# Moving the last gating steps between the tiles of an expert layer, and one to three tiles earlier, in a fused attention and mixture-of-experts kernel

## The chip, the cores and the metric

One core of a Trainium2 chip. The metric is the device time of one execution in microseconds; lower is better. It is taken as the median of several executions.

## The reference, cut to what matters

Two layers in float32 over 32 sequences of 128 tokens, width 128: cross attention with 16 heads to a context of 77 tokens, then a feed-forward layer of 8 experts of which each token takes the best 2.

```python
x = x + xattn(layernorm(x), ctx, ctx, W_q, b_q, W_k, b_k, W_v, b_v, W_o, b_o, mask)
n = layernorm(x)
pn = l2norm(n @ Wp.T);  sn = l2norm(sim_matrix)
gate_scores = pn @ sn.T / temperature
top_v, top_i = top_k(gate_scores, 2)
comb = sum(one_hot(top_i) * softmax(top_v)[..., None], axis=-2)
h  = gelu(n @ W1[e] + b1[e])            # for each expert e
eo = h @ W2[e] + b2[e]
x = x + sum_e eo[e] * comb[..., e]
```

## The kernel before, in words

The attention runs over 16 pairs of sequences (J = 0 to 15, NP = 16), as a software pipeline in which each engine has its own written order (step). At the end of a pair's pipeline stand the gating steps. TensorE turns the normalised rows (turn), multiplies them with the gate weights (gate) and counts how many earlier tokens chose the same expert (rank, count_rows). ScalarE copies and squares (turned, gated). VectorE adds the attention's result to x (residual), takes its mean and variance (second_stats, second_mean), normalises it into rows (second_norm), picks the best two experts (gates, best, best_places, one_hots, chosen, chosen_sum, chosen_sums) and makes from the ranks the row numbers in the experts' lists (ranks, rows_of_lists, rows_taken). GpSimd takes the powers -1/2 (second_power for the norm, gate_power for the gate's length, signalled as rn_ready) and scatters each pair's rows, four indirect DMAs per pair, into lists in DRAM (scatter).

Then 71 tiles of 128 rows (N_TILES = 71) go through the expert layer. Tile j uses the weights of one expert, whose number comes from a table. The tables are made in two parts: part 0, for the first 41 tiles, before the tiles start, and part 1 from the counts of all pairs, in 14 small VectorE stages (tables(1, stage)), one step on TensorE (tables(1)) and the copies back on VectorE (table_rows(1), which ends with the instruction into tab_b that brings tab_ready to 5). The attention's last pairs are not done when the tiles start: the gating of pairs 14 and 15 and the tables of part 1 run among tiles 0 to 20.

Each engine has a function for one tile. An engine works through its instructions in the order written, and a wait holds up all that stands behind it.

- TensorE, tile(j): transpose the rows of tile j+2 (L767), the 8 "up" matmuls of tile j+1 (L774, they wait for xtT of j+1, w1c of j+1 and h of j-1), the 8 "down" matmuls of tile j-1 (L785, they wait for hT of j-1 and eo of j-3).
- VectorE, tile(j): eo of tile j-1 (L1703, after its down), the copy xtT of tile j+3 (L1709, after its transpose), then h of tile j+2 (L1725, after its up).
- ScalarE, tile(j): the weight copy w1c of tile j+2 (L1189), then the gelu hT of tile j (L1193).
- GpSimd, give_back(j): the row numbers didx of tile j+1 (places, L579), then the indirect DMA that scatters eo of tile j into results (L590), then a memset that spaces these DMAs (L593). A list scatter (L457) among them is followed by a longer memset (spread, L527).
- SyncE loads the rows of a tile into a ring of 8 buffers: tile j+8 is loaded when didx of tile j has been computed and its rows were transposed (L395 to L399).

The helper steps (L315) calls between(j) ahead of tile(j) for the tiles up to the start of its loop; the loop starts at tile 20 on VectorE, 21 on TensorE and ScalarE, 22 on GpSimd. On TensorE, ScalarE and GpSimd the gating steps are in between(j) before the change. On VectorE they are in beside(j), which tile(j) calls in its middle, after the copy xtT and ahead of h (L1710). TensorE and ScalarE wait for tab_ready = 5 ahead of their tile 21, VectorE ahead of its tile 20.

Of the kernel before, what the change touches and what calls it, by code (L numbers as in the profile page):

```python
# [6 lines left out]
def xattn_moe_kernel(nc, x, ctx, mask, w_q, b_q, w_k, b_k, w_v, b_v, w_o, b_o,  # L7
# [26 lines left out]
    NP = NB // 2  # L34
# [26 lines left out]
    LOOPED = 20  # L61
# [15 lines left out]
    with est:  # L77
# [207 lines left out]
        def known(b):  # L285
            return isinstance(b, int)
# [17 lines left out]
        def settled(eng):  # L304

            eng.nop(nofuse=True)
# [113 lines left out]
        def _(pool):  # L421
# [173 lines left out]
            def between(j):  # L595
                if j == 0:
                    second_power(NP - 1, NP - 1)
                elif j in (7, 9, 11, 13):
                    k = (7, 9, 11, 13).index(j)
                    scatter(NP - 2, NP - 2, k // TOPK, k % TOPK)  # L600
                    spread(5 + k)
                elif j == 6:
                    gate_power(NP - 1, NP - 1)
                    destinations(NP - 1, NP - 1)
                elif j in (15, 17, 19, 21):
                    k = j // 2 - 7
                    scatter(NP - 1, NP - 1, k // TOPK, k % TOPK)
                    spread(9 + k)
                elif j == LOOPED + 2:
                    pool.wait_ge(skip_ready, 2)  # L610
# [17 lines left out]
        def _(pe):  # L628
# [424 lines left out]
            project(15)  # L1053

            def between(j):
                if j == 4:
                    after(pe, E["dots_ready"], NP - 2)
                    rank(NP - 2, NP - 2)
                elif j == 5:
                    after(pe, E["x2_ready"], NP - 1)  # L1060
                    turn(NP - 1, NP - 1)
                elif j == 6:
                    after(pe, E["rk_ready"], NP - 2)
                    gate(NP - 1)
                elif j == 12:
                    after(pe, E["dots_ready"], NP - 1)
                    count_rows(NP - 1, ps_x[:, COUNTED])
                    rank(NP - 1, NP - 1)
                elif j == 20:
                    after(pe, E["xn2T_ready"], NP - 1)  # L1070
                    tables(1)
                elif j == 21:
                    pe.wait_ge(tab_ready, 5)
# [5 lines left out]
        def _(act):  # L1079
# [224 lines left out]
            tile(0, 0)  # L1304

            def between(j):
                if j == 5:
                    turned(NP - 1)
                elif j == 7:
                    gated(NP - 1, NP - 1)  # L1310
                elif j == LOOPED + 1:
                    act.wait_ge(tab_ready, 5)
# [29 lines left out]
        def _(dve):  # L1342
# [49 lines left out]
            def residual(J):  # L1392
                after(dve, E["o_done"], J)
                after(dve, E["xb_ready"], J)
                nc.vector.tensor_tensor(pair(x2, J), ps_o[:, 256:512], pair(x2, J), ALU.add).then_inc(E["x2_ready"], 1)  # L1395
# [65 lines left out]
            def best_places(J):  # L1461
                after(dve, E["top_ready"], J)
                settled(dve)
                for s in range(2):
                    last = nc.vector.max_index(idx8[:, s, :], top8[:, s, :], gv[:, s, :])
                last.then_inc(E["idx_ready"], 1)
                dcol = diff[:, 2 * J:2 * J + 2] if known(J) else diff[:, bass.ds(J * 2, 2)]
                nc.vector.tensor_tensor(dcol, top8[:, :, 1], top8[:, :, 0], ALU.subtract).then_inc(E["diff_ready"], 1)

            def one_hots(J):  # L1470
                after(dve, E["idx_ready"], J)
                nc.vector.tensor_tensor(ohs[:, :, :, :], iota_e[:, 0:NE].unsqueeze(1).unsqueeze(1).to_broadcast([P, 2, TOPK, NE]),
                                        idx8[:, :, 0:TOPK].unsqueeze(3).to_broadcast([P, 2, TOPK, NE]), ALU.is_equal
                                        ).then_inc(E["ohs_ready"], 1)
# [164 lines left out]
                nc.vector.scalar_tensor_tensor(x2[:, b, :], ys[:, b // CH, 1, b % CH, :], p2[:, b:b + 1], x2[:, b, :],  # L1639
                                               ALU.mult, ALU.add).then_inc(sum2, 1)  # L1640

            def beside(j):
                if j == 0:
                    best_places(NP - 2)
                    one_hots(NP - 2)
                elif j == 1:
                    residual(NP - 1)
                    second_stats(NP - 1)
                    second_mean(NP - 1, NP - 1)
                elif j == 2:  # L1650
                    chosen(NP - 2)
                    chosen_sum(NP - 2, NP - 2)
                    chosen_sums(NP - 2, NP - 2)
                elif j == 3:
                    second_norm(NP - 1, NP - 1)
                elif j == 4:
                    ranks(NP - 2)
                    rows_of_lists(NP - 2)
                    rows_taken(NP - 2, NP - 2)
                elif 5 <= j < 8:  # L1660
                    chances(0, j - 5)
                elif j == 8:
                    gates(NP - 1, NP - 1)
                    best(NP - 1)
                elif j == 9:
                    best_places(NP - 1)
                    one_hots(NP - 1)
                elif j == 10:
                    chosen(NP - 1)
                    chosen_sum(NP - 1, NP - 1)  # L1670
                    chosen_sums(NP - 1, NP - 1)
                elif j == 12:
                    ranks(NP - 1)
                    tables(1, 0)
                    tables(1, 1)
                elif j == 13:
                    rows_of_lists(NP - 1)
                    rows_taken(NP - 1, NP - 1)
                    tables(1, 2)
                elif 14 <= j < 17:  # L1680
                    tables(1, 2 * j - 25)
                    tables(1, 2 * j - 24)
                elif j == 17:
                    tables(1, 9)
                    tables(1, 10)
                    tables(1, 11)
                elif j == 18:
                    tables(1, 12)
                    tables(1, 13)
                elif j == 19:  # L1690
                    table_rows(1)

            def tile(j, m):
                t = j - 1 + AHEAD
                if has(j, -1, N_TILES) or has(t, 0, N_TILES):
                    both = dve.value_load(tab_b[0:1, t:t + 1] if known(t) else tab_b[0:1, bass.ds(t, 1)],
                                          min_val=0, max_val=33 * (NE - 1) * FC)
                    e1, e2 = both % 32, both // 32 * (D // FC)
                if has(j, -1, N_TILES):
                    q = (m - 1) % FRING  # L1700
                    after_dma(dve, returned, j - 1 - FRING, q)
                    after_tile(dve, FE["down_done"], j - 1)
                    nc.vector.tensor_tensor(eo[:, q, :], ps_s[:, 2 + (m - 1) % 2, 0:D], b2s[:, bass.ds(e2, D)], ALU.add  # L1703
                                            ).then_inc(FE["eo_ready"], 1)
                if has(j, 3, N_TILES):
                    r = (m + 1) % 2
                    after_tile(dve, FE["up_done"], j + 1)
                    after_tile(dve, FE["xtT_done"], j + 3)
                    nc.vector.tensor_copy(xtT[:, r, :], turned_rows(j + 3, r)).then_inc(FE["xtT_ready"], 1)  # L1709
                if known(j):  # L1710
                    beside(j)
                if known(j) and N_TILES - EARLY <= j < N_TILES:
                    b = j - (N_TILES - EARLY)
                    if b == 0:
                        dve.wait_ge(p_step, 3)
                    if b % CH == 0:
                        after_y(dve, b // CH)
                    first_sum(b)
                    if b > 0:
                        second_sum(b - 1)  # L1720
                if has(j, 2, N_TILES):
                    r = m % 2
                    after_tile(dve, FE["act_ready"], j)
                    after_tile(dve, FE["up_done"], j + 2)
                    nc.vector.tensor_tensor(h[:, r, :].rearrange("p (c t) -> p c t", c=FC),  # L1725
                                            ps_s[:, r, :].rearrange("p (c t) -> p c t", c=FC),
                                            b1T[:, bass.ds(e1, FC)].unsqueeze(2).to_broadcast([P, FC, P]), ALU.add
                                            ).then_inc(FE["h_ready"], 1)
# [155 lines left out]
            best(14)  # L1884
            context(15)
            tile(0, 0)

            def between(j):
                if j == LOOPED:
                    dve.wait_ge(tab_ready, 5)  # L1890

            steps(dve, tile, 1, N_TILES, LOOPED, N_TILES - EARLY - 1, FRING, between)
# [40 lines left out]
```

## Time and profile before

| | |
|---|---|
| median of 3 executions | 378.75 us (377.77 to 378.83) |
| profiled execution | 377.77 us, span from first to last instruction 376.0 us |
| TensorE (PE) busy | 342.3 us, 91% of the span |
| VectorE (DVE) busy | 306.0 us, 81% |
| ScalarE (ACT) busy | 290.3 us, 77% |
| GpSimd (POOL) busy | 271.9 us, 72% |
| mean granted TensorE clock | 0.978 of full speed |

The profile comes from one execution, the 377.77 us one. Times in its rows count from the first instruction. A row of a timeline gives start, length, engine, line, instruction, and, in brackets, how long the engine sat idle before it and what ended that. The chain of waits follows the last instruction back to what released each step. The attention takes the span up to about 209 us; TensorE's tiles run from there to 353 us, and the remainder is the last results' way back through DRAM and the sum.

### The profile page before, as it was taken

The numbers are of one execution on the slowest core, as the hardware profiler recorded it, in microseconds if no ns is written. First come the engines' busy times: TensorE is split into PE (matmuls) and PEld (weight loads), VectorE is DVE, ScalarE is ACT, GpSimd is POOL, SyncE is SP. The second block draws the span as 40 slices with busy tenths as digits, with TensorE's granted clock in tenths as the row PEclk, the third lists the DMA queues.
The fourth block names the chain that finished last, engine by engine and source line by source line (L and its number), as shares of the span: only waits on it lengthen the run. The fifth ranks groups of instructions, "written<-read, shape, count | busy, mean of one in ns | idle before, by whom it ended". The sixth has DMA issues, their size and how long they took to land.

```text
span 376.0 us, 14240 instructions
## 1 busy us (share of the span) xinstructions
PE 342.3 (91%) x3584; PEld 288.8 (77%) x3585; DVE 306.0 (81%) x972; ACT 290.3 (77%) x847; POOL 271.9 (72%) x506
## 2 busy tenths in 40 slices
PE   7899999999999999999998899999999999999900
PEld 3467777777777777777776699999889999999900
DVE  6778999999999999999999787786556666668884
ACT  4899999999999999999987857665556666666621
POOL 7532487777777877777755468899888878687773
PEclk9999999999999999999999999999999999999965
DMA  3122123321331211120000212222232222249247
GB/s 93 45 82 80 32 72 102 102 64 61 103 97 63 59 44 44 52 72 22 22 25 30 68 45 74 67 68 72 74 86 80 76 71 70 70 133 285 62 117 218
DMA packets 42567, 29.16 MB, mean 78 GB/s; under 512 B 5443, under 2 KB 39311, under 8 KB 42528
## 3 DMA queue, kind: packets, MB, share of 16 engines
q1 hardware_dynamic: 34992, 18.60, 18.3%
q0 software_dynamic: 4320, 8.53, 6.8%
q10 hardware_dynamic: 3216, 1.57, 1.5%
q8 instruction: 16, 0.26, 0.3%
q14 instruction: 23, 0.19, 0.2%
HBM read 17.53 MB, written 11.62 MB: 78 GB/s over the span
## 4 chain that ended last, share of the span: by engine, by line
PE 54%; DVE 22%; issue 10%; POOL 4%; ACT 3%; DMA 3%; DVEq 2%; POOLq 0%; SPq 0%; ACTq 0%
PE ps_s L774 14%; PE ps_s L785 14%; PE ps_t L665 6%; PE ps_o L676 5%; PE ps_s L649 4%; DVE sums L1373 4%; DVE mx L1356 3%; PE ps_s L639 3%; DVE rows L1441 2%; PE ps_t L767 2%; PE ps_x L696 2%; DVE pr L1366 2%; DMA ys<-results 1%; DVE x L1395 1%; DVE st L1405 1%
## 5 line engine op out<-in xcount | busy, mean ns | idle before, releaser
L590 POOL DMA_INDIRECT results<-eo,didx x71 | 70.7, 996 | 19.8 <-issue 13.2
L457 POOL DMA_INDIRECT lists<-rows,slots x64 | 66.7, 1042 | 17.8 <-issue 16.4
L785 PE MATMUL ps_s<-w2s,hT 128*128 x568 | 75.8, 277 | 0.1
L774 PE MATMUL ps_s<-xtT,w1c 128*128 128x128 f32 x568 | 75.5, 276 | 0.0
L1091 ACT ACTIVATE pT<-ps_t 77x512 f32<-77x512 f32 x128 | 73.8, 594 | 0.9 <-PE ps_t L665 0.9
L665 PE MATMUL ps_t<-identf,pr 128*77 128x128 f32 x512 | 72.7, 275 | 0.4 <-ACT pT L1091 0.3
L785 PEld LDWEIGHTS ps_s<-w2s,hT 128*128 128x128 f32 x568 | 69.1, 192 | 0.8 <-issue 0.4
L1189 ACT ACTIVATE w1c<-w1s 128x512 f32 x71 | 44.7, 630 | 31.9 <-PE ps_s L774 29.4
L774 PEld LDWEIGHTS ps_s<-xtT,w1c 128*128 128x128 f32 x568 | 69.0, 192 | 0.1
L1725 DVE TENSOR_TENSOR h<-ps_s,b1T 128x512 f32<-128x512 f32 x71 | 49.1, 691 | 19.4 <-PE ps_s L774 18.7
L665 PEld LDWEIGHTS ps_t<-identf,pr 128*77 128x77 f32 x512 | 58.6, 147 | 6.8 <-issue 4.6
L1193 ACT ACTIVATE hT<-h 128x512 f32<-128x512 f32 x71 | 44.7, 629 | 18.5 <-DVE h L1725 14.2
L1356 DVE TENSOR_REDUCE mx<-ps_s 128x8 f32<-128x616 f32 x64 | 48.1, 792 | 8.4 <-PE ps_s L649 8.3
L1366 DVE TENSOR_TENSOR pr<-ps_s,mx 128x308 f32<-128x308 f32 (+1 forms) x64 | 40.1, 630 | 0.1
L1131 ACT ACTIVATE pr<-ps_s,mx 128x77 f32<-128x77 f32 x128 | 39.8, 329 | 0.4 <-DVE mx L1356 0.2
L1703 DVE TENSOR_TENSOR eo<-ps_s,b2s 128x128 f32<-128x128 f32 x71 | 20.7, 292 | 23.0 <-PE ps_s L785 17.7
L676 PE MATMUL ps_o<-pT,vpad 77*32 77x128 f32 x1024 | 34.6, 276 | 4.0 <-ACT recT L1179 4.0
L1373 DVE TENSOR_REDUCE sums<-pr 128x12 f32<-128x924 f32 x32 | 35.4, 1105 | 0.0
L676 PEld LDWEIGHTS ps_o<-pT,vpad 77*32 77x32 f32 x1024 | 26.0, 109 | 10.6 <-ACT recT L1179 7.6
L520 POOL TENSOR_TENSOR kbd<-kT,headmask 128x616 f32<-128x616 f32 x16 | 19.4, 1213 | 15.4 <-ACT kT L1155 15.3
L1131 ACT ACTIVATION_READ_ACCUMULATOR pr<-ps_s,mx 128x1 f32 x128 | 26.9, 210 | 0.0
L649 PE MATMUL ps_s<-kbd,qT 32*128 32x308 f32 x256 | 25.6, 470 | 0.4 <-ACT qT L1173 0.4
(220 smaller groups left out, 621.3 us busy)
## 6 DMA issues: line engine op xcount, KB each, us to landing
xt<-lists SPq DMA_DIRECT2D x71, 66.0 KB, 1.9
ys<-results SPq DMA_DIRECT2D x14, 256.0 KB, 4.0
xin<-in_x_dram SPq DMA_DIRECT2D x16, 128.0 KB
w1s<-in_L_ffn_W_dram SPq DMA_DIRECT2D x8, 256.0 KB
w2s<-in_L_ffn_W_dram SPq DMA_DIRECT2D x8, 256.0 KB
out_dram<-x SPq DMA_DIRECT2D x5, 256.0 KB, 6.0
cin<-in_ctx_dram SPq DMA_DIRECT2D x16, 77.0 KB
results<-eo,didx POOLq DMA_INDIRECT x71, 2.4
```

Of the source, the lines that this page charges most:

```text
L457: nc.gpsimd.indirect_dma_start(lists, bass.IndirectOffsetOnAxis(ap=slots[:, r, s * TOPK + k:s * TOPK + k + 1], axis=0), rows[:, r, s, k, : ...
L590: nc.gpsimd.indirect_dma_start(results, bass.IndirectOffsetOnAxis(ap=didx[:, r:r + 1], axis=0), eo[:, r, :], None, bounds_check=TOPK * NTO ...
L665: last = nc.tensor.transpose(ps_t[0:SK, g % 2, j * P:(j + 1) * P], pr[:, s, g * HG + j, :], identf[:, :])
L676: last = nc.tensor.matmul(ps_o[g * QR:(g + 1) * QR, s * P:(s + 1) * P], vpad[0:SK, r, s * G + g, j * QR:(j + 1) * QR], pT[0:SK, g, j * P:( ...
L774: last = nc.tensor.matmul(ps_s[:, r, c * P:(c + 1) * P], w1c[:, r, c * P:(c + 1) * P], xtT[:, r, :], start=True, stop=True)
L785: last = nc.tensor.matmul(ps_s[:, 2 + r, 0:D], hT[:, r, c * P:(c + 1) * P], w2s[:, bass.ds(e + c * D, D)], start=(c == 0), stop=(c == FC - 1))
L1091: nc.scalar.activation(pT[0:SK, g, :], ps_t[0:SK, g % 2, :], ACT.Copy).then_inc(E[f"t{g}_ready"], 1)
L1131: last = nc.scalar.activation(pr[:, s, hd, :], ps_s[:, 3, (hd - HB) * SK:(hd - HB + 1) * SK], ACT.Exp, bias=mx[:, s, hd:hd + 1], accum_out ...
L1356: nc.vector.tensor_reduce(grouped(mx[:, s, n * HG:(n + 2) * HG]), bank(n, 2), AX.X, ALU.max, negate=True).then_inc(E["maxA" if n == 0 else ...
L1366: nc.vector.tensor_tensor(pr[:, s, hd, :].rearrange("p (n h) k -> p n h k", h=HG), bank(n, nb), grouped(mx[:, s, hd]).unsqueeze(3).to_broa ...
L1373: nc.vector.tensor_reduce(sums[:, m % 2, s, 0:HB], pr[:, s, 0:HB, :], AX.X, ALU.add).then_inc(E["sums_ready"], 1)
L1725: nc.vector.tensor_tensor(h[:, r, :].rearrange("p (c t) -> p c t", c=FC), ps_s[:, r, :].rearrange("p (c t) -> p c t", c=FC), b1T[:, bass.d ...
```

## The change: what it does

VectorE's function beside is taken away. Its steps go into between(j), ahead of the whole tile(j), so that they stand behind h of the tile before instead of ahead of h of this tile. Those of pair 14's choice (best_places to chosen_sums) and pair 15's residual, statistics and mean all come right behind tile(0). The second norm of pair 15 moves from tile 3 to ahead of tile 2, the row numbers of pair 14 from tile 4 to ahead of tile 3, chances from 5 to 7 to ahead of 4 to 6. The steps from gates(15) on keep their number j and stand ahead of the tile; the tables' stages are dealt out anew, and table_rows(1) goes from the middle of tile 19 to ahead of tile 20.

TensorE's rank(14), turn(15), gate(15) and count_rows and rank(15) come one tile earlier, as do ScalarE's turned(15) and gated(15). GpSimd's scatters of pair 14 go from ahead of tiles 7, 9, 11, 13 to ahead of 3, 4, 7, 9, and those of pair 15 from 15, 17, 19, 21 to 14, 16, 18, 20. Its gate_power(15) stays ahead of tile 6.

```diff
 GpSimd, between(j)
-                elif j in (7, 9, 11, 13):
-                    k = (7, 9, 11, 13).index(j)
+                elif j in (3, 4, 7, 9):
+                    k = (3, 4, 7, 9).index(j)
                     scatter(NP - 2, NP - 2, k // TOPK, k % TOPK)
                     spread(5 + k)
                 elif j == 6:
                     gate_power(NP - 1, NP - 1)
                     destinations(NP - 1, NP - 1)
-                elif j in (15, 17, 19, 21):
+                elif j in (14, 16, 18, 20):
 TensorE, between(j)
-                if j == 4:
+                if j == 3:
                     after(pe, E["dots_ready"], NP - 2)
                     rank(NP - 2, NP - 2)
-                elif j == 5:
+                elif j == 4:
                     after(pe, E["x2_ready"], NP - 1)
                     turn(NP - 1, NP - 1)
-                elif j == 6:
+                elif j == 5:
                     after(pe, E["rk_ready"], NP - 2)
                     gate(NP - 1)
-                elif j == 12:
+                elif j == 11:
                     after(pe, E["dots_ready"], NP - 1)
                     count_rows(NP - 1, ps_x[:, COUNTED])
                     rank(NP - 1, NP - 1)
 ScalarE, between(j)
-                if j == 5:
+                if j == 4:
                     turned(NP - 1)
-                elif j == 7:
+                elif j == 6:
                     gated(NP - 1, NP - 1)
 VectorE, tile(j)
-                if known(j):
-                    beside(j)
 VectorE, after tile(0, 0)
+            best_places(14)
+            one_hots(14)
+            chosen(14)
+            chosen_sum(14, 14)
+            chosen_sums(14, 14)
+            residual(15)
+            second_stats(15)
+            second_mean(15, 15)
 
             def between(j):
-                if j == LOOPED:
+                if j == 2:
+                    second_norm(NP - 1, NP - 1)
+                elif j == 3:
+                    ranks(NP - 2)
+                    rows_of_lists(NP - 2)
+                    rows_taken(NP - 2, NP - 2)
+                elif 4 <= j < 7:
+                    chances(0, j - 4)
+                elif j == 8:
+                    gates(NP - 1, NP - 1)
+                    best(NP - 1)
+                elif j == 9:
+                    best_places(NP - 1)
+                    one_hots(NP - 1)
+                elif j == 10:
+                    chosen(NP - 1)
+                    chosen_sum(NP - 1, NP - 1)
+                    chosen_sums(NP - 1, NP - 1)
+                elif j == 12:
+                    ranks(NP - 1)
+                    tables(1, 0)
...
+                elif j == LOOPED:
+                    table_rows(1)
                     dve.wait_ge(tab_ready, 5)
```

## Rows read from the trace of the kernel before

**Rows 1.** Windows: stretch, length, busy us of each engine, PE clock, DMA share, GB/s
```profile
223.00:256.00 33.00, 32.79 (x292) 32.32 (x292) 26.37 (x97) 21.79 (x40) 29.26 (x56) 1.00 0.25 71
256.00:276.00 20.00, 18.32 (x149) 17.11 (x148) 10.79 (x31) 10.24 (x18) 18.05 (x35) 1.00 0.24 70
276.00:300.00 24.00, 24.00 (x215) 23.81 (x214) 14.73 (x37) 15.69 (x26) 21.17 (x45) 1.00 0.30 84
```

**Rows 2.** Chain that ended last, around 271 to 274 us: start, length, what
```profile
271.29 0.15 POOL didx L579
...
272.32 1.86 DMA xt<-lists
...
274.23 0.33 PE ps_t L767
```

**Rows 3.** Timeline of GpSimd (POOL): start, length, instruction, idle time before it and its releaser
```profile
221.61 0.19 POOL L496 TENSOR_SCALAR ve<-mv 128x2 f32<-128x2 f32 x1 [2.10 <-DVE mv L1414]
...
222.94 1.05 POOL L590 DMA_INDIRECT results<-eo,didx  x1 [0.17 <-POOL didx L579]
...
226.24 0.99 POOL L590 DMA_INDIRECT results<-eo,didx  x1 [0.16 <-DVE eo L1703]
...
231.55 0.99 POOL L590 DMA_INDIRECT results<-eo,didx  x1 [0.58 <-issue]
...
233.27 0.72 POOL L509 TENSOR_TENSOR rn<-n2c,neghalf 128x2 f32<-128x2 f32 x1
...
239.41 1.00 POOL L590 DMA_INDIRECT results<-eo,didx  x1 [0.16 <-POOL didx L579]
...
242.63 0.99 POOL L590 DMA_INDIRECT results<-eo,didx  x1 [0.16 <-DVE eo L1703]
```

**Rows 4.** Timeline of VectorE (DVE), tiles 0 to 2
```profile
218.13 0.08 DVE L1465 MATCH_VALUE_LOAD idx<-top,gv 128x8 f32 x1
...
218.77 0.69 DVE L1725 TENSOR_TENSOR h<-ps_s,b1T 128x512 f32<-128x512 f32 x1
...
220.01 0.41 DVE L1395 TENSOR_TENSOR x<-ps_o,x 128x256 f32<-128x256 f32 x1
...
221.45 0.69 DVE L1725 TENSOR_TENSOR h<-ps_s,b1T 128x512 f32<-128x512 f32 x1
...
222.70 0.17 DVE L1479 TENSOR_TENSOR sel<-ohs 128x16 bf16<-128x16 f32 x1
```

**Rows 5.** Timeline of TensorE (PE); L767 opens a tile
```profile
221.11 1.06 PE L774 MATMUL ps_s<-xtT,w1c 128*128 128x128 f32 x8
...
223.28 0.17 PE L702 MATMUL ps_x<-sel,tri 128*128 128x16 bf16 x1 [0.21 <-DVE selsum L1485]
...
231.97 0.27 PE L767 MATMUL ps_t<-identf,xt 128*128 128x128 f32 x1
...
233.86 0.27 PE L767 MATMUL ps_t<-identf,xt 128*128 128x128 f32 x1
...
239.82 0.30 PE L767 MATMUL ps_t<-identf,xt 128*128 128x128 f32 x1
...
255.65 0.28 PE L767 MATMUL ps_t<-identf,xt 128*128 128x128 f32 x1
...
280.57 0.27 PE L767 MATMUL ps_t<-identf,xt 128*128 128x128 f32 x1
```

**Rows 6.** Timeline of VectorE, tiles 8 and 19
```profile
234.64 0.48 DVE L1451 TENSOR_SCALAR gv<-dots,rn 128x8 f32<-128x8 f32 x2
...
256.24 0.17 DVE L1602 TENSOR_SCALAR bias_at<-ps_o 1x33 f32<-1x33 f32 x1
...
256.69 0.17 DVE L1612 SCALAR_TENSOR_TENSOR tab_b<-bias_at 1x33 int32<-1x33 f32 x1
257.07 0.69 DVE L1725 TENSOR_TENSOR h<-ps_s,b1T 128x512 f32<-128x512 f32 x1 [0.20 <-PE ps_s L774]
```

**Rows 7.** Timeline of ScalarE (ACT), tile 21
```profile
257.82 0.63 ACT L1189 ACTIVATE w1c<-w1s 128x512 f32 x1 [1.75 <-DVE tab_b L1612]
```

More of the change, by code:

```diff
@@ L1640, in second_sum @@
                                                ALU.mult, ALU.add).then_inc(sum2, 1)
[L1642 to L1691, printed above, removed]
             def tile(j, m):
@@ L1886, in _ @@
             tile(0, 0)
-            def between(j):
-                if j == LOOPED:
+            best_places(14)
[6 more added lines that the diff above has]
+            second_mean(15, 15)
+            def between(j):
+                if j == 2:
[19 more added lines that the diff above has]
+                    tables(1, 0)
+                elif j == 13:
+                    rows_of_lists(NP - 1)
+                    rows_taken(NP - 1, NP - 1)
+                    tables(1, 1)
+                elif 14 <= j < 17:
+                    tables(1, 2 * j - 26)
+                    tables(1, 2 * j - 25)
+                elif 17 <= j < 19:
+                    tables(1, 3 * j - 43)
+                    tables(1, 3 * j - 42)
+                    tables(1, 3 * j - 41)
+                elif j == LOOPED:
+                    table_rows(1)
                     dve.wait_ge(tab_ready, 5)
```

## The prediction

> **What bounds the kernel now.** I read the windows first, then the chain, then the timelines of the four engines over tiles 0 to 30. I write P8 for the start of TensorE's tile 8, its L767 row; G5 for the start of GpSimd's L590 of tile 5; a dash (P8') for the same thing after the change. The windows split the edited region in two [rows 1]. From 223 to 256 us TensorE is busy 32.79 of 33 us: it never waits for VectorE there, and a tile costs 233.86 - 231.97 = 1.895 us [rows 5]. From 256 to 276 it is busy 18.32 of 20, while GpSimd has 18.05; after 276 it is full again up to the last tile. The chain says what the waits of the middle window are [rows 2]: didx of tile 22 on GpSimd at 271.29, then the load of tile 30, which lands at 274.18, then TensorE's tile 28. GpSimd had been working without a break from 221.61, where it had waited 2.10 us for the mean of pair 15 [rows 3]. So the ring of 8 buffers, paced by GpSimd, sets TensorE's time at tile 28, and TensorE, which with 1.895 us a tile would have been there earlier, has slack before it. From P12 = 239.82 to P20 = 255.65 are 15.83 us [rows 5]; 8 more tiles of 1.895 would bring P28 to 270.8. It came at 274.23 [rows 2]: the slack is 3.4 us. The time after P31 = 280.57 [rows 5] follows TensorE one to one. The change's worth is therefore the shift of P31.
>
> **The GpSimd chain.** It starts with the mean of pair 15. VectorE's rows price the moved steps, from one start to the next [rows 4]: the places and one-hots 218.77 - 218.13 = 0.64 us; the three chosen steps 0.65 (222.70 to TensorE's rank at 223.28, which needs two of them [rows 5], and a third like them, an estimate); residual, statistics and mean 221.45 - 220.01 = 1.44. Before, h of tile 2 stood behind the places and started at 218.77; now it starts at 218.13 and takes 0.62, then come 0.64 + 0.65 + 1.44. The mean is ready at 221.5 us instead of 221.45. Nothing is gained there: the chosen steps that went ahead of it cost what tile 1's eo and xtT cost before. The work on GpSimd's queue up to G21 stays the same: 22 returns at (226.24 - 222.94) / 2 = 1.65 us or a little less, 8 scatters that each make 1.6 more (242.63 - 239.41 = 3.22 with one [rows 3]), and gate_power. All eight stand ahead of G21 in both orders. The only term is the 0.58 us of idle time ahead of G5 [rows 3], of which 0.4 is beyond the usual; it may go or stay. So the ring allows P28' between 273.8 and 274.3.
>
> **VectorE, tiles 0 to 6.** The xtT copy of tile 4 used to be done for TensorE's up at 221.11 [rows 5]; now it stands behind all the steps of the last paragraph: mean at 221.5, about 0.4 for register work, eo, then xtT, done near 222.4. TensorE waits 1.3 us. It wins back the wait at rank(14) (223.28, [rows 5]), since chosen is done by 220.1. Then up and down of tile 3 take 1.8, and turn, gate and two tiles as before (P6 = 231.97 - 2 x 1.895 = 228.18, less 223.28, less 0.2 for rank, 4.7): P6' = 222.45 + 1.8 + 4.7 = 228.95, which is 0.8 late. The moves of second_norm and of ranks(14) cost nothing: their inputs are there 1 us ahead, and an op of up to 1.1 us between h and eo delays xtT by less than TensorE has in hand.
>
> **The order of gates(15).** GpSimd now has two scatters ahead of G3 and G4, and gate_power(15) still stands ahead of G6. G5' = G2 + 3.22 + 3.22 + 1.63 = 226.24 + 8.07 = 234.3, against 231.55. The power ends 233.27 + 0.72 - 231.55 = 2.44 behind it [rows 3]: 236.75, against 233.99. VectorE's gates(15) stand ahead of its tile 8, where VectorE arrives at 234.9 (P8' = 232.75, and h comes 1.4 us behind the tile's start: 257.07 - 255.65 [rows 5, 6]), so it waits 2 us with eo of tile 7, xtT of tile 11 and h of tile 10 queued behind. gates take 0.48 (L1451, [rows 6]) and best with the gaps about as much again, 0.85 together as an estimate, then eo, then xtT at 238.7. TensorE wanted it at P10' = 228.95 + 4 x 1.895 = 236.5. It waits 2.1 us, so P10' acts as 238.65. Before, the same wait had 0.65 in hand (gates at 234.64 [rows 6] against 233.99).
>
> **The order of count_rows(15).** TensorE wants the three chosen sums at the end of tile 10 (ahead of tile 11). VectorE does them ahead of its tile 10, which is behind h of tile 11, and that h needs TensorE's up of tile 10. So: P10' + 1.4 (h) + 0.6 + 0.65 + 0.15 = P10' + 2.8, where TensorE is free at P10' + 1.9. That is a wait of 0.9 whatever came before, and the places of pair 15, still late from the last paragraph, add about 0.4. P11' = 238.65 + 2.8 + 0.4 + 0.3 (count and rank) = 242.15, P12' = 244.1, P20' = 244.1 + 15.83 = 259.9.
>
> **The order of table_rows.** Before, it took 256.24 to 256.86, ahead of h of tile 21 at 257.07 [rows 6], and TensorE's tile 21, at P20 + 1.9 = 257.55, came behind it and did not wait. Now it is behind that h: P20' + 1.42 + 0.62 + 0.62 = P20' + 2.66. TensorE, free at P20' + 1.9, waits for it ahead of its tile 21 and then has the loop's head and its register work to do, which took ScalarE 257.82 - 256.86 = 0.96 [rows 6, 7]; I take 0.45 for TensorE, between 0.15 (a bare wake-up) and 0.96. P21' = P20' + 3.1 = 263.0. w1c of tile 23 comes at P20' + 3.6 and is wanted at P20' + 5: hidden.
>
> **The sum.** P31' = 263.0 + 10 x 1.895 = 281.95, and about 0.25 for the first tile behind a wait, which runs slower (P12 to P20 before held 0.1 of it): 282.2, against 280.57. The shift is +1.6 us. The ring asks only for 274.3 at P28' (276.3 here), so it no longer binds. The profiled execution would go from 377.77 to 379.4, the median, 0.98 above it before, from 378.75 to 380.35. I say 380.3.
>
> **The rivals.** (B) TensorE's waits are covered by its slack. They sum to 0.8 + 2.1 + 1.3 + 1.2 = 5.4 against 3.4 of slack and 0.6 of slow tiles that went with the waits before. If gates(15) finds its power 1.5 us sooner, or the loop heads are free, P28' is the ring's 274.2 and the time 378.7. For: the sum exceeds the slack by little, and each term is worked out to some 0.3 us. Against: three terms would have to be too large at once. (D) Faster: the waits stay small, GpSimd's 0.4 us goes, and TensorE, with no wait at tile 28, skips the slow tiles that followed it (280.57 - 274.23 = 6.34 for three tiles of 1.895, 0.65 lost). P31' = 273.8 + 5.7 = 279.5, time 377.7. It decides where the power of pair 15 is done by 235 us. Against: GpSimd had no idle time from which the scatters could be paid. (C) Slower: the waits reach GpSimd. Its return at 226.24 was released by eo of tile 2 [rows 3], and VectorE is late there by up to 0.8 us; with that the power, gates and all behind move too, and each wait leaves 0.4 of slow tiles: +3, 381.8. (E) The TensorE clock falls in a wait and 2 to 3 tiles run at half speed: +4 to +6 us beside the rest, near 384.5. The rows speak against it: the granted clock stayed at 1.00 through the window with 1.68 us of waits [rows 1], though none alone was as long as 2 us.
>
> The Trainium skill (TensorE: Matmul & The Clock Gate, Part 1, "What's actually happening") says that an idle TensorE is set back to 1.2 GHz, the lower of two levels, and that activity releases it; by that rule (E) is possible if a wait counts as idle, and gives its 384.5. No row here has a wait of 2 us inside the tiles, so the trace leaves it open; the window at 1.00 is nearest and I follow it.
>
> **How the numbers follow.** Chances: forecast 0.55 (own range 379.4 to 381.4), B 0.23, C 0.11, D 0.07, E 0.04. A measurement of this kernel tells about 0.3% (1.1 us) from no change. Slower by more: four fifths of the forecast, C and E, 0.6. Faster: half of D and the tail of B, 0.07. The remaining 0.33 is the same. The range goes from B's low side, 378.2, to C's 381.9.
>
> **What would show it.** Right: VectorE idle 1.5 to 2.5 us ahead of gv (L1451) with the power on GpSimd as releaser; TensorE waiting near 241 us for the sums ahead of L709 and for tab_b ahead of tile 21; no wait for xt loads at tiles 22 to 28; P31 near 282. Wrong: if TensorE still waits for xt at tile 28 near 274, the ring has kept the bound; if P6 is before 228.2 or gv has no wait, my order of arrival is wrong.

## The result and the profile after

The changed kernel takes 384.2 us (383.54 to 385.56) against 378.69 for the kernel before; the ratio is 1.0155, 95% interval 1.0119 to 1.0191. It is 5.5 us slower, where 1.6 were forecast; the range ended at 381.9. The profiled execution took 386.43 us, its span is 384.6; it is the slowest of the eleven executions of this measurement (382.83 to 386.43), so its rows show more of a loss than the median does.

TensorE of the kernel after (start, length, instruction, idle time before it and its releaser). Against [rows 5]:

```profile
224.23 1.16 PE L774 MATMUL ps_s<-xtT,w1c 128*128 128x128 f32 x8 [1.48 <-DVE xtT L1658]
...
238.24 0.27 PE L767 MATMUL ps_t<-identf,xt 128*128 128x128 f32 x1
241.18 1.16 PE L774 MATMUL ps_s<-xtT,w1c 128*128 128x128 f32 x8 [2.66 <-DVE xtT L1658]
242.26 1.87 PE L785 MATMUL ps_s<-w2s,hT 128*128 x8
244.64 0.17 PE L709 MATMUL ps_x<-selsum,onesb 128*128 128x8 bf16 x1 [0.51 <-DVE selsum L1490]
...
245.17 1.94 PE L774 MATMUL ps_s<-xtT,w1c 128*128 128x128 f32 x8
...
250.85 0.27 PE L767 MATMUL ps_t<-identf,xt 128*128 128x128 f32 x1
...
266.45 0.28 PE L767 MATMUL ps_t<-identf,xt 128*128 128x128 f32 x1
...
269.52 0.32 PE L767 MATMUL ps_t<-identf,xt 128*128 128x128 f32 x1 [0.94 <-DVE tab_b L1612]
...
288.91 0.27 PE L767 MATMUL ps_t<-identf,xt 128*128 128x128 f32 x1
```

The first row is the up of tile 4 (the matmuls of L774), which stood at 221.11 before; it waits 1.48 us for xtT. At 241.18 the up of tile 11 waits 2.66 us; behind it the groups of eight take 1.87 and 1.94 us where they took 1.06. L709 waits for the sums, the transpose at 269.52 for tab_b, and P31 is 288.91 against 280.57. No transpose waits for a load at tiles 22 to 28 any more.

VectorE of the same kernel, against [rows 4, 6]:

```profile
222.83 0.25 DVE L1414 BATCH_NORM_AGGREGATE mv<-st 128x2 f32<-128x6 f32 x2
223.69 0.29 DVE L1652 TENSOR_TENSOR eo<-ps_s,b2s 128x128 f32<-128x128 f32 x1 [0.61 <-issue]
...
225.34 0.28 DVE L1652 TENSOR_TENSOR eo<-ps_s,b2s 128x128 f32<-128x128 f32 x1
...
239.31 0.36 DVE L1451 TENSOR_SCALAR gv<-dots,rn 128x8 f32<-128x8 f32 x2 [2.75 <-POOL rn L509]
...
240.63 0.29 DVE L1652 TENSOR_TENSOR eo<-ps_s,b2s 128x128 f32<-128x128 f32 x1 [0.62 <-issue]
...
257.99 0.15 DVE L1564 TENSOR_TENSOR upto<-done,todo 128x16 f32<-128x16 f32 x1
258.78 0.29 DVE L1652 TENSOR_TENSOR eo<-ps_s,b2s 128x128 f32<-128x128 f32 x1 [0.63 <-issue]
...
260.25 0.16 DVE L1571 TENSOR_REDUCE which<-cmp 128x1 f32<-128x16 f32 x1
261.05 0.29 DVE L1652 TENSOR_TENSOR eo<-ps_s,b2s 128x128 f32<-128x128 f32 x1 [0.64 <-issue]
```

gv (L1451) waits 2.75 us for the power. A row that the forecast had not: eo (L1652) stands 0.6 us in "issue", time in which the engine waits for nothing that the profile shows, behind most of the moved steps (223.69, 240.63, 258.78, 261.05). Behind the second norm, whose instruction takes 0.73 us, it does not (225.34).

GpSimd, against [rows 3]: the chain starts at 223.27, the return of tile 2 at 228.68 (G2'), that of tile 5 at 236.76 (G5', forecast 234.3), the power at 238.49.

```profile
223.27 0.19 POOL L496 TENSOR_SCALAR ve<-mv 128x2 f32<-128x2 f32 x1 [2.72 <-DVE mv L1414]
...
228.68 0.99 POOL L590 DMA_INDIRECT results<-eo,didx  x1 [0.56 <-issue]
...
236.76 0.99 POOL L590 DMA_INDIRECT results<-eo,didx  x1 [0.16 <-issue]
...
238.49 0.72 POOL L509 TENSOR_TENSOR rn<-n2c,neghalf 128x2 f32<-128x2 f32 x1
```

The windows, against [rows 1]; columns as there, the granted clock third from the end:

```profile
223.00:256.00 33.00, 28.60 (x225) 27.92 (x226) 18.72 (x70) 16.43 (x32) 26.61 (x51) 0.90 0.22 60
256.00:276.00 20.00, 18.36 (x151) 16.76 (x150) 13.12 (x48) 10.67 (x18) 17.42 (x33) 1.00 0.24 67
```

From 223 to 256 TensorE has 28.60 of 33 us where it had 32.79, and 225 matmuls instead of 292: it waits 4.2 us more, and its clock is at 0.90 of full speed. Four shorter windows show where:

```profile
238.00:241.00 3.00, 0.52 (x5) 0.28 (x3) 0.96 (x6) 0.31 (x1) 2.65 (x7) 1.00 0.16 44
241.00:244.00 3.00, 2.82 (x16) 2.55 (x16) 2.32 (x12) 1.26 (x2) 2.67 (x5) 0.75 0.24 70
244.00:247.00 3.00, 2.49 (x14) 2.33 (x14) 0.91 (x6) 0.63 (x1) 2.67 (x6) 0.50 0.31 89
247.00:250.00 3.00, 3.00 (x19) 3.00 (x19) 1.18 (x3) 1.26 (x2) 2.14 (x6) 0.61 0.27 65
```

From 244 to 247 us the granted clock is 0.50, the lower level, 1.2 GHz; TensorE had waited 2.66 us before it fell.

TensorE's tile starts in the two profiled executions place the loss:

| stretch | before | after | difference | forecast |
|---|---|---|---|---|
| up to P3 | 221.00 | 222.45 | +1.45 | 0 |
| P3 to P9 | 12.86 | 13.90 | +1.04 | +0.8 |
| P9 to P13 | 7.95 | 14.50 | +6.55 | +3.4 |
| P13 to P20 | 13.84 | 15.60 | +1.76 | 0 |
| P20 to P21 | 1.90 | 3.07 | +1.17 | +1.2 |
| P21 to P31 | 23.02 | 19.39 | -3.63 | -3.8 |
| sum at P31 | | | +8.34 | +1.6 |

The first line lies ahead of every instruction that the change moves: TensorE's tiles start 0.7 us later (210.56 against 209.86) and the first load of rows comes 0.7 later still. It is left out of the account. In the four profiles of the changed kernel and its versions taken next the tiles start 0.4 to 0.7 us later than in the one profile of the kernel before, so whether all of it is chance stays open.

### The profile page after: what moved, and what is told of

The parts are those of the page before. It is cut to its first block, busy times and chain, and to the rows that moved or that the text cites. A ratio compares the mean times of both kernels' runs of the same rounds, so it can differ in the third digit from the quotient of the medians.

```text
span 384.6 us, 14240 instructions
## 1 busy us (share of the span) xinstructions
PE 346.2 (90%) x3584; PEld 291.7 (76%) x3585; DVE 305.0 (79%) x972; ACT 290.7 (76%) x847; POOL 272.2 (71%) x506
## 4 chain that ended last, share of the span: by engine, by line
PE 52%; DVE 24%; issue 11%; POOL 3%; ACT 3%; DVEq 3%; DMA 3%; SPq 1%; POOLq 0%; ACTq 0%
PE ps_s L774 14%; PE ps_s L785 13%; PE ps_t L665 6%; PE ps_o L676 4%; DVE sums L1373 3%; PE ps_s L649 3%; DVE mx L1356 3%; PE ps_s L639 2%; DVE rows L1441 2%; DVE h L1672 2%; PE ps_t L767 2%; PE ps_x L696 1%; DMA ys<-results 1%; DVE pr L1366 1%; DVE x L1395 1%
## 5 line engine op out<-in xcount | busy, mean ns | idle before, releaser
L774 PE MATMUL ps_s<-xtT,w1c 128*128 128x128 f32 x568 | 77.0, 279 | 4.8 <-DVE xtT L1658 4.6
L785 PE MATMUL ps_s<-w2s,hT 128*128 x568 | 76.9, 280 | 0.1
L774 PEld LDWEIGHTS ps_s<-xtT,w1c 128*128 128x128 f32 x568 | 70.2, 195 | 6.3 <-DVE xtT L1658 6.2
L785 PEld LDWEIGHTS ps_s<-w2s,hT 128*128 128x128 f32 x568 | 70.6, 196 | 0.6 <-issue 0.4
L1652 DVE TENSOR_TENSOR eo<-ps_s,b2s 128x128 f32<-128x128 f32 x71 | 20.7, 292 | 28.6 <-issue 14.3
```

Source lines behind the costliest of these rows:

```text
L774: last = nc.tensor.matmul(ps_s[:, r, c * P:(c + 1) * P], w1c[:, r, c * P:(c + 1) * P], xtT[:, r, :], start=True, stop=True)
L785: last = nc.tensor.matmul(ps_s[:, 2 + r, 0:D], hT[:, r, c * P:(c + 1) * P], w2s[:, bass.ds(e + c * D, D)], start=(c == 0), stop=(c == FC - 1))
```

## The experiments

The runs were made in five series, each with the kernel before beside the others. Ratios are to the kernel before of the same series, with 95% intervals. In the first series (after_again to load_first) the kernel before took 379.0 us, and the parts can be priced to 0.5 us. In the other four it took 387 to 394. The chains of nine of the fourteen traces taken there hold pauses of 1.1 to 4.4 us that no instruction explains (no trace of the kernel before was taken there); those series tell only what is larger than some 0.3%.

**The control, after_again.** No edit.

> The changed kernel once more, as control for the runs beside it. Theory (four costs add up: VectorE's wait for the power of pair 15, 2.8 us; the TensorE clock that falls in that wait, about 2.8; register work of VectorE that lies open behind each moved step, about 2.3; the waits for the chosen sums and for tab_b, about 2): 384.2, with the same waits at the same tiles. Rival (part of the 5.5 us is scatter between executions, as the attention ended 0.7 us later in the one profile taken): this profile lies at 383 or less, with the attention as before.

386.16 us where 384.2 were expected, before 378.98: ratio 1.019 (1.0174 to 1.0205). The waits stand at the same tiles to 0.02 us. The rival falls: its tiles start 0.4 us late in the profile, and the loss was larger, 7.2 us. All executions here had a mean granted clock of 0.969 or 0.970. Of the eleven of the first measurement, the four at 0.970 or 0.971 took 385.6 to 386.4, the seven at 0.975 to 0.978 took 382.8 to 384.6.

**fill: keep TensorE busy in the wait.**

```diff
+                elif j == 10:
+                    warm_up(10)
                 elif j == 11:
```

> The changed kernel with ten matmuls of 512 columns on the constant ones, into a bank that nobody reads then, on TensorE ahead of its tile 10, where it otherwise waits 2.8 us for xtT of tile 11. Theory (the fall of the clock behind that wait is a cost of its own): the wait of VectorE's gv for the power stays at about 2.8 us, the granted clock stays at 1.00, the groups of 8 behind it take 1.06 instead of 1.87 to 1.94, and the time falls by 2.5 to 3 us to 381.5. Rival (VectorE and GpSimd set the pace there, the slow matmuls are covered): groups at 1.06 but the time stays within 0.5 us of 384.2.

383.92 us, 2.2 less than the control; ratio 1.0128 (1.0108 to 1.0149). TensorE of this kernel:

```profile
237.08 2.32 PE L931 MATMUL ps_o<-onesb 128*128 128x512 bf16 x10
...
240.10 1.16 PE L774 MATMUL ps_s<-xtT,w1c 128*128 128x128 f32 x8 [0.59 <-DVE xtT L1660]
241.19 1.15 PE L785 MATMUL ps_s<-w2s,hT 128*128 x8
243.57 0.17 PE L709 MATMUL ps_x<-selsum,onesb 128*128 128x8 bf16 x1 [1.23 <-DVE selsum L1492]
```

and its window 244 to 247, with the clock at 1.00 where it was 0.50:

```profile
244.00:247.00 3.00, 3.00 (x28) 3.00 (x28) 1.67 (x5) 1.26 (x2) 2.67 (x6) 1.00 0.25 75
```

The groups of eight matmuls are back at 1.1 and P9 to P13 takes 12.54 us instead of 14.50. The fall of the clock is a cost of its own, 2 us in executions like those of the control; the 2.5 to 3 expected were a little high, as a second wait, 1.23 us at L709 instead of 0.51, took some back.

**pool_order: the scatters of pair 14 back.**

```diff
-                elif j in (3, 4, 7, 9):
-                    k = (3, 4, 7, 9).index(j)
+                elif j in (7, 9, 11, 13):
+                    k = (7, 9, 11, 13).index(j)
```

> The changed kernel with GpSimd's scatters of pair 14 back ahead of tiles 7, 9, 11 and 13, so that gate_power(15) is no longer behind two of them. Theory: gv's wait of 2.8 us goes, with it the idle stretch in which the clock fell, and about 0.4 us at the chosen sums: 6 us less if nothing else binds, of which the ring and the remaining waits leave about 4 us: 380.3. Rival (the order of the scatters is not the cause, the late start of GpSimd's chain behind the mean of pair 15 is): gv still waits over 1 us and the time stays above 383.

380.56 us, 5.6 less than the control, 0.3 from the expected time; ratio 1.0044 (1.003 to 1.0058). The power comes at 234.69 (GpSimd) and gv no longer waits (VectorE):

```profile
234.69 0.72 POOL L509 TENSOR_TENSOR rn<-n2c,neghalf 128x2 f32<-128x2 f32 x1
```

```profile
235.52 0.36 DVE L1451 TENSOR_SCALAR gv<-dots,rn 128x8 f32<-128x8 f32 x2
```

The rival falls, and the order of the scatters is shown as the cause of the long wait. P9 to P13 takes 9.79 us. TensorE's tiles 16 to 18 still take 2.3 to 2.5 us each.

**load_first: the steps behind the register read.**

```diff
                     e1, e2 = both % 32, both // 32 * (D // FC)
+                if known(j):
+                    ahead_of_eo(j)      # the steps of between(j), 2 <= j < 19
```

> The changed kernel with VectorE's steps of between(j) done inside tile(j), behind the read of the expert's offset from tab_b into a register and ahead of eo, instead of ahead of that read. Same steps, same places against eo, xtT and h. Theory (behind a step the register read lies open, 0.6 us per tile, and makes VectorE's tiles 15 to 20 2.3 to 2.4 us long, above TensorE's 1.895): the idle time of 0.6 ahead of eo goes in those tiles, TensorE's tiles 16 to 19 are back at 1.9, and the time falls by 2 to 2.5 us to about 382. Rival (the steps themselves are too long to fit behind h): tiles of 2.3 stay, the time falls by less than 0.5.

380.14 us, 6.0 less than the control where 2 to 2.5 were expected; ratio 1.0032 (1.0018 to 1.0047). VectorE of this kernel, behind the last steps ahead of two tiles:

```profile
252.44 0.15 DVE L1564 TENSOR_TENSOR upto<-done,todo 128x16 f32<-128x16 f32 x1
252.59 0.29 DVE L1688 TENSOR_TENSOR eo<-ps_s,b2s 128x128 f32<-128x128 f32 x1
...
254.19 0.16 DVE L1571 TENSOR_REDUCE which<-cmp 128x1 f32<-128x16 f32 x1
254.30 0.29 DVE L1688 TENSOR_TENSOR eo<-ps_s,b2s 128x128 f32<-128x128 f32 x1
```

eo follows 0.15 and 0.11 us behind the start of the last step, against 0.79 and 0.80 in the kernel after (257.99 to 258.78, 260.25 to 261.05). P13 to P20 takes 13.84 us, exactly the time of the kernel before: 1.76 of the 6.0. Most of the rest is in P9 to P13, 11.01 instead of 14.50 (0.9 came ahead of tile 9, 0.5 of it ahead of tile 3, where the code is the same), and TensorE's rows say why it is more than the 0.6 of one register read:

```profile
238.80 1.16 PE L774 MATMUL ps_s<-xtT,w1c 128*128 128x128 f32 x8 [1.71 <-DVE xtT L1694]
239.79 1.06 PE L785 MATMUL ps_s<-w2s,hT 128*128 x8
```

The up of tile 11 waits 1.71 us instead of 2.66: the power came 0.35 us sooner against the tile's start (gv waits 2.42 instead of 2.75), and from gv to eo are 0.70 us instead of 1.32. The groups behind the wait take 1.16 and 1.06: the clock stayed up in all four executions (0.978 to 0.980). So part of the 6.0 is the clock's 2 us, which fill had priced. Stretch by stretch against the kernel before, in the order of the table above, load_first has +0.41, +0.65, +3.06, 0, +1.15 and -3.73, and P31 at 282.11, where the forecast had 282.2.

**order_load: both edits at once**, in three series, as they were disturbed.

> The changed kernel with both of the last two edits: scatters of pair 14 back ahead of tiles 7 to 13, and VectorE's steps behind the register read. Theory (the costs of the order on GpSimd and of the open register read are separate terms): tiles 17 to 19 on TensorE go from 2.3 to 2.5 us back to 1.9, 1.6 us in all, on top of the 5.6 that the order gave: 378.9, what is left over being the wait for xtT of tile 4, the chosen sums and tab_b, under the ring's slack. Rival (the two edits repair the same loss, each took 5.6 to 6 us alone): 380.1, no better than either.

> The kernel with both edits (scatters of pair 14 back, steps behind the register read) again: in the last call the kernel before itself took 393.7 instead of 378.9, and engines stood still up to 5 us in places that no wait of the program explains, so its differences of 1 us could not be read. Theory (order and register read are separate terms): before + 0 to 0.3, 379.0. Rival (they repair the same loss): 380.1, before + 1.2.

> Scatters of pair 14 back and VectorE's steps behind the register read. Theory A (separate terms): before + 0 to 0.3, as nothing over the ring's slack is left. Theory B (both repair the same loss, the idle stretch in which the clock fell, and the rest is the waits for the sums and tab_b): before + 1.2, as each alone.

Ratios 1.0039 (1.001 to 1.0068), 1.006 (1.0032 to 1.0088) and 1.0037 (1.0017 to 1.0057), medians 395.04, 395.9 and 388.74. Theory A, before + 0.3 at most, is outside all three intervals. Theory B, before + 1.2 (1.003), is inside two and just below the third: the two edits repair mostly the same loss, the long wait with the clock's fall behind it, and 1.3 to 2.6 us stay above before. How much of that is these series' own pauses is not told apart.

**all_back: both edits, and with them count_rows(15) and rank(15) ahead of tile 12 and table_rows(1) in the middle of tile 19.**

```diff
-                elif j == 11:                    # TensorE
+                elif j == 12:
+                if known(j) and j == LOOPED - 1: # VectorE, tile(j), behind xtT
+                    table_rows(1)
```

> As the kernel with both edits, and with count_rows and rank of pair 15 back ahead of TensorE's tile 12 and table_rows(1) back in the middle of VectorE's tile 19. Theory (the waits of 0.9 to 1.2 us for the chosen sums and of 1.2 us for tab_b are the last two terms; behind them the ring, paced by GpSimd, binds as in the kernel before): TensorE's tiles 11 and 21 at 1.9, waits for xt near tiles 22 to 28 again, 378.9 to 379.1, equal to before. Rival (the waits were all that held it, and the earlier placing pays): 1.5 us below before, 377.4.

> The kernel with all four edits again, for the same reason. Theory (nothing but the ring is left): equal to before within 0.3 us, with waits for xt near tiles 22 to 28. Rival (early placing pays): 1.5 us below before.

> All four edits. Theory: the waits for the sums (0.9) and for tab_b (1.2) go, TensorE's tiles 11 and 21 take 1.9 to 2.2; where h2 was above before by them, this is equal to before within 0.3, and the ring binds again. Rival: 1.5 below before.

> All four edits, beside it. Theory: equal to start_only within 0.3 us, since only the start is left of the change's costs. Undisturbed, both are at before + 0 to 0.3.

Ratios 1.0018 (0.9991 to 1.0046), 1.0029 (1.0006 to 1.0053), 1.0033 (1.001 to 1.0056) and 1.0019 (0.9999 to 1.004). Each is 0.2 to 0.3% above before, two of them clear of noise and two not: the rival, that the earlier placing pays 1.5 us, falls, and the theory, equal to before within 0.3 us (0.0008), is inside three of the intervals and just outside the other. What the waits for the sums and for tab_b cost alone is not told apart here, since order_load and all_back overlap in all three series in which both ran.

**pool_only: GpSimd's part of the change alone on the kernel before.**

```diff
-                elif j in (7, 9, 11, 13):
+                elif j in (3, 4, 7, 9):
-                elif j in (15, 17, 19, 21):
+                elif j in (14, 16, 18, 20):
```

> The kernel before with GpSimd's part of the change alone: all eight scatters where the change has them. Theory (the late power costs what stands behind VectorE's wait for it; in the old place, in the middle of tile 8, eo of tile 7 and xtT of tile 11 are already done and only h of tile 10 is behind it): gv waits about 2 us, TensorE waits 0.5 us or less, the slack covers it: 379.0, the same as before. Rival (the late power is enough by itself): TensorE waits 2 us near its tile 10, the clock falls, 381 or more.

> GpSimd's part of the change alone on the kernel before, again. Theory (only what stands behind VectorE's wait counts, and in the middle of tile 8 that is h alone): gv waits about 2 us, TensorE at tiles 10 and 11 about 0.5, and the time is before within 0.3. Rival (the late power is enough): TensorE waits 2 us and more and the time is before + 2. In the disturbed call gv waited 1.7 and the time was equal to before.

Ratios 0.9983 (0.9954 to 1.0011) and 0.9992 (0.9973 to 1.001): no difference, as expected. In the two profiles gv waited 1.72 and 0.48 us, less than the 2.75 of the kernel after. TensorE's up of tile 12 in the second waited 0.45 us:

```profile
242.35 1.16 PE L774 MATMUL ps_s<-xtT,w1c 128*128 128x128 f32 x8 [0.45 <-DVE xtT L1709]
```

In the first it waited 1.00. So the new order of the scatters costs nothing that can be measured where only h stands behind gv, and in the changed kernel, where eo and xtT do, taking it back gave 5.6 us. These series are those with the pauses; the chain of the first profile shows one, on VectorE between a register instruction and the next wait:

```profile
256.14 0.02 DVEq L1696
256.17 2.27 another core or an unknown queue
...
258.46 0.02 DVEq L294
```

**no_spread: the kernel before without the spacing memsets.**

```diff
                     scatter(NP - 2, NP - 2, k // TOPK, k % TOPK)
-                    spread(5 + k)
...
-                    spread(9 + k)
```

> The kernel before without the eight spacing memsets (spread) behind the list scatters of pairs 14 and 15, 0.46 us each on GpSimd's chain. Theory (GpSimd's queue, through the ring of 8 buffers, holds TensorE at tiles 22 to 28): the chain is 3.7 us shorter, the waits for xt go, TensorE's tiles 22 to 30 take 1.9 and the time falls by 3 to 4 us to 375.3. Rival (the spacing is needed, closer scatters make the DMAs or the instruction issue slower by as much, or TensorE is the bound): 378 to 379.

> The kernel before without the eight spacing memsets behind list scatters, again. Theory (GpSimd's chain through the ring binds): 375.3. Rival (without the spacing GpSimd's DMA issues slow down, as the disturbed call had it, 5 us above before with 18 us of idle time of GpSimd ahead of its returns): before or above, 379 to 384.

> The kernel before without the eight spacing memsets behind list scatters. Theory (GpSimd's chain through the ring binds in an undisturbed execution): 3 to 4 us below before, TensorE's tiles 22 to 28 at 1.9. Rival (seen in two disturbed calls: GpSimd stands 1.3 to 2.8 us ahead of some returns once the spacing is gone): 0 to 4 us above before.

Ratios 1.0111 (1.0079 to 1.0142), 1.0108 (1.0081 to 1.0135) and 1.0163 (1.0118 to 1.0209). The theory falls for these executions: it is slower, by 4.6 to 6 us. GpSimd of the last, two returns:

```profile
248.74 1.00 POOL L590 DMA_INDIRECT results<-eo,didx  x1 [2.26 <-issue]
...
257.84 1.00 POOL L590 DMA_INDIRECT results<-eo,didx  x1 [1.97 <-issue]
```

With the 0.46 us memset gone, three returns up to 260 us stand 1.2 to 2.8 us in "issue" in each of the three traces; up to 260 us no other trace of these series has one over 1.4. But the chain that ended last goes through something else. In all three traces it holds a pause of 4.1 to 4.4 us on VectorE behind the last of pair 15's chosen sums, which is most of the loss; in the last:

```profile
242.18 4.33 another core or an unknown queue
```

In the other eleven traces of these series no pause on the chain is over 2.4 us. What it is, and whether GpSimd's issues or this pause cost the time, was not tested, and no undisturbed series has this version, so whether GpSimd's chain can be shortened is open.

**start_only: the steps right behind tile 0, alone on the kernel before**; and the changed kernel in a disturbed series.

```diff
             tile(0, 0)
+            best_places(14)
+            one_hots(14)
...
+            second_mean(15, 15)
```

> The kernel before with one part of VectorE's move alone: places, one-hots and chosen of pair 14 and residual, statistics and mean of pair 15 right behind tile 0; all else in its old place. Theory: TensorE's step from tile 3 to tile 4 takes 3.2 to 3.6 us instead of 2.4 (4.4 where registers are slow), GpSimd's chain starts 0.2 us later; the ring covers the first and leaves 0.2: before + 0 to 0.3 us undisturbed, and + 1 where the disturbed chips have no slack. Rival (the start costs nothing, what was left in all_back is the register read): before within 0.1% on any chip.

> The changed kernel as control beside the three others. Theory: before + 5.5 to 7, depending on how long the clock stays low in an execution.

start_only: ratio 0.9995 (0.9964 to 1.0026), its ten executions from 390.4 to 397.3; two of them, at a mean clock of 0.969, took 396.7 and 397.3, above every execution of the kernel before (392.2 to 395.2). That shows no cost in the median, but the interval ends at + 1.0 us: the theory's + 1 is at its very edge and the + 0 to 0.3 of an undisturbed chip well inside, so neither it nor the rival is settled (all_back beside it stood 1.0 us higher, within the noise of both), and what makes the 0.2 to 0.3% of all_back stays open. h1_after: 390.33 against 387.43, ratio 1.0075 (1.0048 to 1.0103), 2.9 us, less than the 5.5 to 7 expected; its clock was low for two groups of eight, behind a wait of 2.55 us, and TensorE's tile 11 took 1.98 us instead of 3.67.

## Why the prediction was wrong, step by step

- **The GpSimd chain**: right at its start and in the order. It started at 223.27 instead of 221.61, 1.66 us later, of which 1.39 is the late start of the tiles (P2 220.50 against 219.11), where the forecast had 0.05 for the remainder; from G2' to G5' it took 8.08 us, forecast 8.07. But from its start to G2' it took 5.41 us instead of 4.63, and the forecast had kept the 4.63. G2' stands 1.10 us behind the start of eo of tile 2 (227.58), as it does in after_again, fill and pool_order, and 0.56 us idle where 0.16 is usual, so about half of this 0.8 is VectorE's late eo; in load_first, where eo came sooner, it is 5.00 us. That is the mechanism of rival (C), at 0.8 us instead of its 3.
- **VectorE, tiles 0 to 6**: right, +1.04 against +0.8. The wait for xtT of tile 4 was 1.48 us, forecast 1.3.
- **The order of gates(15)**: right in mechanism and place. gv waited 2.75 us on the power (forecast 2), TensorE 2.66 (2.1); the excess is the 0.8 of the paragraph above. pool_order shows the cause.
- **The clock**: this is one of the two steps that failed. The forecast priced a wait at its own length and the clock behind it at nothing; rival (E) was given 4%, held down by a window whose 1.68 us of waits came in pieces. The clock fell: granted clock 0.50 from 244 to 247 us, three groups of eight at 1.87 to 1.94 us and one at 1.30, 2.0 to 2.2 us by fill. Rival (E) had priced it at 4 to 6 us, for 2 to 3 whole tiles. The Trainium skill (TensorE: Matmul & The Clock Gate, Part 1, "What's actually happening") says that an idle TensorE is set back to 1.2 GHz; the trace agrees, with 0.50 of full speed behind a wait of 2.66 us.
- **"An op of up to 1.1 us between h and eo delays xtT by less than TensorE has in hand"**: this is the other step that failed. The 1.1 were counted without the read of the expert's offset from tab_b. Before, that read (L1696) ran while h was in the engine and ended with it, as the chain of the kernel before shows:

```profile
221.45 0.34 DVE h L1725
...
221.83 0.19 DVEq L1696
...
222.12 0.12 DVEq L1703
...
222.29 0.06 DVE eo L1703
```

```profile
257.88 0.19 DVE cum L1563
258.08 0.07 DVEq L1645
...
258.24 0.19 DVEq L1645
...
258.61 0.13 DVEq L1652
...
258.78 0.06 DVE eo L1652
```

From 258.08 to eo at 258.78 are 0.7 us. With it VectorE's own loop is eo 0.2, xtT 0.2, h 0.6, steps 0.6 to 0.8 and 0.6 to 0.7 of read, 2.2 to 2.5 us (from eo at 258.78 to eo at 261.05 are 2.27), and VectorE sets the pace of tiles 16 to 19: +1.76 us, which load_first gives back exactly. It also lengthened the wait at tile 11, by 0.95 against load_first, where the clock stayed up. That the length of the wait decided this was not tested by itself.
- **The order of count_rows(15)**: right in kind, forecast 1.3 us. In the kernel after it was hidden in part by the slow clock (0.51 us ahead of L709); in pool_order it is 1.23.
- **The order of table_rows**: right, P20 to P21 is 3.07, forecast 3.1.
- **The ring's slack**: right, 3.63 us given back, forecast 3.8, and no waits for xt at tiles 22 to 28.
- **The sum**: 1.6 forecast. With 1.76 for the open read, 2 for the clock and about 1.1 for the longer waits between P9 and P13 it is 6.5, against 6.9 at P31 without the first line of the table, and 5.5 (7.2 in the control) in the medians. load_first is the kernel that the forecast had in mind: with the read back under h and the clock up each of its stretches comes within 0.4 us of the forecast's, and its median is 1.2 us above before, forecast 1.6. So the other terms were sound; that P31 meets the forecast to 0.1 us is luck, since 0.41 us of it is the late start and the waits at tiles 4 and 11 were 0.15 and 0.4 us shorter than forecast.

## What to carry to other kernels

Work moved behind an engine's last long instruction is not as cheap as the same work ahead of it: what the sequencer did under that instruction, here a 0.6 us register read, comes into the open, on every tile with such a step. When a step's consumer is another engine's in-order queue, check each producer of that step for what its own queue now has ahead of it, and what stands behind the wait; the same order of scatters cost 5.6 us with eo behind the wait and nothing measurable with only h behind it. A forecast wait on TensorE that is longer than any in the rows should carry the price of a slow clock behind it, with a chance of its own.

## What the runs showed of the hardware

TensorE's granted clock went to 0.50 behind a wait of 2.66 us in the kernel after and to 0.55 (242 to 245 us) behind one of 2.55 in h1_after, and stayed at 1.00 behind one of 1.71 in load_first; ten matmuls in the gap kept it at 1.00. The length of a single wait does not decide it alone. Behind the same wait of 1.96 us for xtT of tile 4 it stayed at 1.00 in h3_all_back and k2_all_back and fell to 0.50 (227 to 229 us) in d2_all_back:

```profile
225.55 1.16 PE L774 MATMUL ps_s<-xtT,w1c 128*128 128x128 f32 x8 [1.96 <-DVE xtT L1694]
```

Behind one of 1.95 in b1_order_load it fell to 0.50 (260 to 262 us), behind one of 2.09 in k1_start_only it stayed at 1.00 (277 to 282 us). What else decides was not tested. The cost differed between executions of one kernel too: of the kernel after, those at a mean clock of 0.970 or 0.971 took about 2.5 us more than those at 0.975 and above. No version tried here beats the kernel before.
